# A two-layer adapter and feed-forward kernel: another order of loads, remainders and one fold in its opening

## The reference, cut to what matters

```python
# layer 0, x is 2 x 2048 x 512; domain_id holds one number for each of the 2 batches
hidden = gelu(x @ down_W.T + down_b)                       # 512 -> 128
expert_out = hidden @ expert_W[idx].T + expert_b[idx]      # one expert for each batch
hidden = where(valid, expert_out, hidden) + domain_emb[idx]
x = layernorm(hidden @ up_W.T + up_b + x) * ln_gamma + ln_beta
# layer 1
h = gelu(x @ Wi[e] + bi[e])                                # 512 -> 2048, one expert for each batch
o = h @ Wo[e] + bo[e]                                      # 2048 -> 512
return layernorm(o + x) * gamma[e] + beta[e]
```

## Time and profile before

| what | value |
|---|---|
| median of 3 runs | 768.83 us (768.16 to 769.0) |
| time of the profiled execution | 767.69 us |
| its span (first to last instruction) | 765.9 us |
| PE busy | 755.4 us, 99% of the span |
| DVE busy | 514.1 us, 67% |
| POOL busy | 466.9 us, 61% |
| ACT busy | 348.9 us, 46% |
| share of PE in the chain that ended last | 97% |

### The profile page before, as it was taken

The page is one execution under the profiler, slowest core; times in us unless marked ns, Lnnn a source line. Parts: engine busy times, 40 slices in busy tenths (PEclk is TensorE's granted clock), DMA queues, the critical chain, the costliest instruction groups (busy, mean ns, idle before and its releaser), DMA issues.

```text
span 765.9 us, 9925 instructions
## 1 busy us (share of the span) xinstructions
PE 755.4 (99%) x3388; PEld 626.3 (82%) x3388; DVE 514.1 (67%) x1056; ACT 348.9 (46%) x609; POOL 466.9 (61%) x398
## 2 busy tenths in 40 slices
PE   8999999999999999999999999999999999999996
PEld 6888888888888888888888888888888888888885
DVE  7717855789458883689837888368873789545116
ACT  6554445434544444544454344454354444443440
POOL 5497564775648665395655955558653775646441
PEclk9999999999999999999999999999999999999999
DMA  8940000310012000246211300022000210001001
GB/s 313 393 154 1 1 0 13 112 41 1 1 67 86 14 1 0 69 142 257 88 50 69 97 1 1 1 97 69 1 1 1 68 42 1 0 15 42 0 1 55
DMA packets 17270, 45.36 MB, mean 59 GB/s; under 512 B 2115, under 2 KB 3395, under 8 KB 16324
## 3 DMA queue, kind: packets, MB, share of 16 engines
q1 hardware_dynamic: 16532, 43.94, 16.0%
q10 hardware_dynamic: 688, 0.79, 0.3%
HBM read 36.33 MB, written 8.39 MB: 58 GB/s over the span
## 4 chain that ended last, share of the span: by engine, by line
PE 97%; DVE 1%; POOL 0%; issue 0%; ACT 0%; POOLq 0%; DVEq 0%
PE acc L832 15%; PE acc L830 15%; PE acc L831 15%; PE ps_h L832 15%; PE ps_h L830 15%; PE ps_h L831 15%; PE ps L831 2%; PE ps L830 2%; PE ps L832 2%; PE ps_h L938 1%; DVE rows L753 0%; DVE acc L746 0%; DVE stats L735 0%; PE ps L931 0%; POOL up_b L352 0%
## 5 line engine op out<-in xcount | busy, mean ns | idle before, releaser
L306 POOL TENSOR_TENSOR wi<-w_raw,wi 128x512 fp32r<-128x512 f32 x128 | 168.0, 1313 | 242.9 <-ACT wi L446 242.3
L467 ACT ACTIVATE h<-ps_h,bi_now 128x512 fp32r<-128x512 f32 x110 | 75.9, 690 | 295.0 <-PE ps_h L832 295.0
L657 DVE TENSOR_TENSOR h<-ps_h,h 128x512 fp32r<-128x512 f32 x124 | 85.5, 690 | 167.0 <-ACT ps_h L468 166.0
L830 PE MATMUL acc<-wo,h 128*128 128x512 f32 x504 | 196.1, 389 | 0.0
L831 PE MATMUL acc<-wo,h 128*128 128x512 f32 x504 | 196.1, 389 | 0.0
L832 PE MATMUL acc<-wo,h 128*128 128x512 f32 x504 | 196.1, 389 | 0.0
L830 PE MATMUL ps_h<-x1t,wi 128*128 128x512 f32 (+1 forms) x504 | 195.3, 387 | 0.0
L831 PE MATMUL ps_h<-x1t,wi 128*128 128x512 f32 (+1 forms) x504 | 195.2, 387 | 0.0
L832 PE MATMUL ps_h<-x1t,wi 128*128 128x512 f32 (+1 forms) x504 | 195.2, 387 | 0.0
L312 POOL TENSOR_TENSOR wo<-w_raw,wo 128x512 fp32r<-128x512 f32 x126 | 162.9, 1293 | 0.0
L646 DVE STREAM_TRANSPOSE ps<-rows 32x128 f32<-32x128 f32 x448 | 144.3, 322 | 5.7
(11 more groups left out here) (157 smaller groups left out, 620.3 us busy)
## 6 DMA issues: line engine op xcount, KB each, us to landing
w_raw<-in_w SPq DMA_DIRECT2D x32, 512.0 KB, 9.0
rows<-in_x SPq DMA_DIRECT2D x32, 256.0 KB, 2.8
out<-rows SPq DMA_DIRECT2D x32, 256.0 KB, 2.0
xt_raw<-in_xT SPq DMA_DIRECT2D x7, 1024.0 KB, 4.8
vec<-in_vec SPq DMA_DIRECT2D x2, 768.0 KB, 8.3
xt_raw<-in_xT ACTq DMA_DIRECT2D x2, 256.0 KB, 4.6
xt_raw<-in_xT SPq DMA_DIRECT2D x2, 256.0 KB, 3.6
vec<-in_vec SPq DMA_DIRECT2D x1, 512.0 KB, 6.4
```

The lines of the kernel that those rows point to most:

```text
L306: pool.tensor_tensor(slot[:, 1], w_raw[:, c, 0, :].rearrange("p (k i) -> p k i", k=KD), slot[:, 0].bitcast(F32), ALU.subtract).then_inc(wi ...
L467: act.activation(h_slot(t, c)[:, 0, :], bank, ACT.Gelu, bias=bias)
L657: dve.tensor_tensor(h_slot(t, c)[:, 1, :], hidden_bank(t, c), h_slot(t, c)[:, 0, :].bitcast(F32), ALU.subtract).then_inc(h_split, 1)
L830: pe.matmul(out, left[0], right[0], start=start, stop=False)
```

## The change

The loads of SP are asked for in another order: the up bias ahead of up_W, rows 0 and 1 ahead of parts 2 and 3 of x transposed. Gamma and beta lie in 128 rows of memory, one for each partition, and no longer in one row that is read 128 times. DVE copies the up bias right after the flags, ahead of the remainders; up_W's remainder comes behind that of part 0. The remainder of part 2 goes from DVE to POOL. ACT rounds part 0 before up_W, and parts 2 and 3 after the fold; batch 1's expert bias is put off. The second place of `WARM` goes from 3 to 1. Batch 1's fold is copied once more by ACT (`fold_copy`, in the memory of `up_raw`), and its remainder is taken by POOL in tile 0, behind `up_bias(1)`, instead of by DVE; PE waits for that remainder only at c == 4 of tile 0. POOL takes the second remainder of wi ahead of `add_up_bias(3)`, and the third and fourth ahead of the inverse roots.

```diff
@@ -43,7 +43,7 @@
 WI_RING, WO_RING, H_RING = 4, 4, 4
 
 UP_AT, NORM_AT, TURN_AT, SPLIT_AT = (4, 6, 8, 10), (5, 7, 9, 11), (6, 8, 10, 12), (7, 9, 11, 13)
-WARM = (4, 3, 4)
+WARM = (4, 1, 4)
 EARLY = 4
 LATE = 6
 
@@ -88,6 +88,7 @@
         ones = rows[:, 1, 1, 0:P]
         one_row = rows[:, 1, 2, :]
         up_b_raw = rows[:, 1, 3, :]
+        fold_copy = rows[:, 1, 0, :]
         valid = sb("valid", [P, 3, BATCH])
         ids = sb("ids", [1, 4, BATCH], I32)
         idx = sb("idx", [1, 2, BATCH], I32)
@@ -139,6 +140,7 @@
         flags_ready, flags_spread = sem("flags_ready"), sem("flags_spread")
         down_landed, up_landed, up_b_landed = sem("down_landed"), sem("up_landed"), sem("up_b_landed")
         up_b_spread, up_b_wide, bias_copied = sem("up_b_spread"), sem("up_b_wide"), sem("bias_copied")
+        fold_copied = sem("fold_copied")
         exp_landed = [sem(f"exp_landed{b}") for b in range(BATCH)]
         vec0_landed = sem("vec0_landed")
         bi_landed = [sem(f"bi_landed{b}") for b in range(BATCH)]
@@ -198,9 +200,9 @@
         @block.sync
         def _(sp):
             sp.dma_start(ids[:, 0:2, :], ids_d.rearrange("p (i b) -> p i b", b=BATCH)).then_inc(ids_landed, 16)
+            sp.wait_ge(const_ready, 4)
+            sp.dma_start(one_row[0:1, :], vec0_d[0:1, 0, :]).then_inc(up_b_landed, 16)
             sp.dma_start(up_raw, upW_d).then_inc(up_landed, 16)
-            sp.wait_ge(const_ready, 4)
-            sp.dma_start(one_row[0:1, :], vec0_d[:, 0, :]).then_inc(up_b_landed, 16)
             sp.wait_ge(idx_ready, 1)
 
             def load_exp(b):
@@ -214,12 +216,12 @@
                 sp.dma_start(rows[:, 0, s, :], x_d[0, s, :, :]).then_inc(rows_landed[s], 16)
 
             load_exp(0)
+            first_rows(0)
+            first_rows(1)
             first_xt(2)
-            first_rows(0)
+            first_xt(3)
             load_exp(1)
-            first_xt(3)
-            first_rows(1)
-            sp.dma_start(vec0[:, :, :], vec0_d[:, 1:3, :].to_broadcast([P, 2, D])).then_inc(vec0_landed, 16)
+            sp.dma_start(vec0[:, :, :], vec0_d[:, 1:3, :]).then_inc(vec0_landed, 16)
             first_rows(2)
             first_rows(3)
             sp.wait_ge(idx_ready, 2)
@@ -245,6 +247,7 @@
             sp.wait_ge(valid_ready, 1)
             sp.wait_ge(up_b_wide, 1)
             sp.wait_ge(up_b_ready, 2)
+            sp.wait_ge(fold_split, 2)
             for s in range(SUB):
                 sp.wait_ge(xb_ready, s + 1)
                 sp.dma_start(rows[:, 1, s, :], x_d[1, s, :, :]).then_inc(rows_landed[s], 16)
@@ -354,7 +357,7 @@
             pool.wait_ge(up_b_wide, 1)
             add_raw_bias(0)
             add_raw_bias(1)
-            pool.wait_ge(first_split, 3)
+            first_rest(2)
             first_rest(3)
             inverse_root(0, 0, 0)
             up_bias(0)
@@ -362,12 +365,12 @@
             add_up_bias(0, 0, 2, 0)
             inverse_root(0, 0, 1)
             wi_rest(0, 0)
+            wi_rest(0, 1)
             add_up_bias(0, 0, 3, 0)
-            wi_rest(0, 1)
+            wi_rest(0, 2)
             inverse_root(0, 0, 2)
-            wi_rest(0, 2)
+            wi_rest(0, 3)
             inverse_root(0, 0, 3)
-            wi_rest(0, 3)
             wo_rest(0, 0)
             wo_rest(0, 1)
             pool.wait_ge(ffn_landed[0], 16)
@@ -379,6 +382,9 @@
                         wi_rest(*ahead(t, bt, bu, c + WI_AHEAD)[::2])
                     if c == 1 and isinstance(t, int) and t == 0:
                         up_bias(1)
+                        pool.wait_ge(fold_copied, 1)
+                        pool.tensor_tensor(fold_w[:, 1, 1, :], fold_copy, fold_w[:, 1, 0, :].bitcast(F32),
+                                           ALU.subtract).then_inc(fold_split, 1)
                     if c in (1, 2, 3, 4):
                         if isinstance(t, int) and t == 0:
                             add_out_bias(0, 0, c - 1, 0)
@@ -491,29 +497,31 @@
                 act.wait_ge(bias_done, b + 1)
                 act.activation(up_b[:, b, :], bank, ACT.Copy).then_inc(bias_copied, 1)
 
+            first_round(0)
             act.wait_ge(up_landed, 16)
             act.activation(up_w[:, 0, :], up_raw, ACT.Copy).then_inc(up_w_hi, 1)
-            first_round(0)
             first_round(1)
             expert_round(0)
             expert_bias(0)
-            first_round(2)
             first_hidden(0, half_hi)
             fold_round(0)
             expert_round(1)
+            first_round(2)
             first_round(3)
             copy_bias(0, acc[:, 3, :])
-            expert_bias(1)
             first_hidden(2, hid_hi)
             wi_round(0, 0, 0)
             x1t_round(0, 0, 0)
+            wi_round(0, 0, 1)
             fold_round(1)
-            wi_round(0, 0, 1)
+            act.wait_ge(up_w_ready, 1)
+            act.activation(fold_copy, fold_bank(1), ACT.Copy).then_inc(fold_copied, 1)
             x1t_round(0, 1, 0)
             wi_round(0, 0, 2)
             wi_round(0, 0, 3)
             for c in range(WO_AHEAD):
                 wo_round(0, 0, c)
+            expert_bias(1)
             x1t_round(0, 2, 0)
             x1t_round(0, 3, 0)
             xt_round(1, 0)
@@ -709,18 +717,17 @@
                               ALU.subtract).then_inc(down_w_ready, 1)
             dve.wait_ge(flags_spread, 1)
             dve.tensor_copy(valid[:, 0:2, :], ps0[:, 1, 0:2 * BATCH].rearrange("p (i b) -> p i b", b=BATCH)).then_inc(valid_ready, 1)
+            dve.wait_ge(up_b_spread, 1)
+            dve.tensor_copy(up_b_raw, acc[:, 0, :]).then_inc(up_b_wide, 1)
+            first_rest(0)
             dve.wait_ge(up_w_hi, 1)
             dve.tensor_tensor(up_w[:, 1, :], up_raw, up_w[:, 0, :].bitcast(F32), ALU.subtract).then_inc(up_w_ready, 1)
-            first_rest(0)
             first_rest(1)
             dve.wait_ge(exp_hi, 1)
             dve.wait_ge(valid_ready, 1)
             expert_rest(0)
-            dve.wait_ge(up_b_spread, 1)
-            dve.tensor_copy(up_b_raw, acc[:, 0, :]).then_inc(up_b_wide, 1)
-            first_rest(2)
-            dve.wait_ge(first_split, 3)
-            dve.sem_inc(xt_split, 3)
+            dve.wait_ge(first_split, 2)
+            dve.sem_inc(xt_split, 2)
             first_hid_rest(0, half_hi, half_split)
             fold_rest(0)
             dve.wait_ge(exp_hi, 2)
@@ -766,7 +773,6 @@
             first_hid_rest(2, hid_hi, hid_split)
             first_scale(1)
             x1t_rest(0, 0, 0)
-            fold_rest(1)
             x1t_rest(0, 1, 0)
             adapter_sum(0, 2, 0, acc_part(2))
             first_stats(2)
@@ -871,7 +877,7 @@
                       k == 0, k == KD - 1).then_inc(down_done, 1)
 
             def first_down(j):
-                if j < 3:
+                if j < 2:
                     pe.wait_ge(first_split, j + 1)
                 else:
                     pe.wait_ge(xt_split, j + 1)
@@ -963,15 +969,15 @@
             bias_product(0, acc[:, 3, :]).then_inc(bias_done, 1)
             first_down(2)
             first_down(3)
+            turn(0)
             fold_product(1)
-            turn(0)
             adapter_up(0, 0, 2, acc[:, 2, :])
             turn(1)
             pe.wait_ge(bias_copied, 1)
             adapter_up(0, 0, 3, acc[:, 3, :])
 
             first_early(1)
-            pe.wait_ge(fold_split, 2)
+            pe.wait_ge(fold_copied, 1)
             for c in range(1, EARLY - 1):
                 early_products(c, 1)
             turn(2)
@@ -997,6 +1003,8 @@
                     if more and c in (0, 1):
                         adapter_down(t + 1, 2 * c)
                         adapter_down(t + 1, 2 * c + 1)
+                    if c == 4 and isinstance(t, int) and t == 0:
+                        pe.wait_ge(fold_split, 2)
                     if more and c in UP_AT:
                         s = UP_AT.index(c)
                         if s:
@@ -1042,8 +1050,8 @@
                                np.asarray(L0_cond_expert_b).reshape(E0, A, 1),
                                np.asarray(L0_cond_domain_emb).reshape(E0, A, 1),
                                np.broadcast_to(np.asarray(L0_cond_down_b).reshape(1, A, 1), (E0, A, 1))], axis=2),
-        "vec0": np.stack([np.asarray(L0_cond_up_b), np.asarray(L0_cond_ln_gamma),
-                          np.asarray(L0_cond_ln_beta)]).reshape(1, 3, D),
+        "vec0": np.broadcast_to(np.stack([np.asarray(L0_cond_up_b), np.asarray(L0_cond_ln_gamma),
+                                          np.asarray(L0_cond_ln_beta)]).reshape(1, 3, D), (P, 3, D)),
         "w": np.concatenate([wi, wo], axis=3),
         "bi": np.asarray(L1_cond_bi).reshape(E1, CH, P).transpose(0, 2, 1),
         "vec1": np.stack([np.asarray(L1_cond_bo), np.asarray(L1_cond_gamma),
```

## The result

The changed kernel takes 771.43 us (median of 7 executions, 769.88 to 773.11), the kernel before, run beside it on the same chip, 768.00 us (7 executions, 767.55 to 769.00). The ratio is 1.0045, with a 95% interval of 1.0032 to 1.0058: slower, by 3.4 us. The profiled execution of the changed kernel took 770.88 us, with a span of 769.1 us. Against the profiled execution before that is 3.19 us more, and 3.2 more in the span.

A forecast was written before the change was run, and what follows sets the result against it. PE was taken to bound the kernel, carrying any opening delay to the end. DVE's order (0.7, with 0.1 for a start behind a wait) and POOL's turns (2.2) gave +3.0 on 768.83: 771.8 us, range 769.4 to 773.3.

The forecast's parts named there:

- What bounds the kernel: PE, 99% busy and dense after the opening; any shift in the opening reaches the end one for one.
- PE's part: Two products fewer ahead of the up bias: its spreading starts 0.86 us earlier, of which 0.41 is left.
- DVE's order without POOL: Copy and up_W ahead of part 1's remainder move its end from 7.72 to 9.44 us; +0.8 counts.
- POOL's turns: POOL's two up bias additions alternate with DVE's remainders, moving part 1's end on to 11.63 us: 2.2 us.
- PE's waits: In the opening PE waits 0.6 us for part 0's remainder and 2.6 for part 1's.
- What was costed at nothing: Fold remainder, part 2 on POOL, wi order, transfers and ACT's extra copy: taken as no cost; up to 0.3 us if ACT late.
- One turn only: Rival, chance 0.10: POOL's first addition runs between up_W's and part 1's remainders; +1.9 us, 770.7.
- rows 0 landing ahead of POOL's asking: Transfers in the opening: rows 0 lands near 7.3 us, before POOL asks at 7.85; taken as no cost.
- POOL costs nothing: Rival, chance 0.07: POOL doesn't delay DVE, part 1's remainder ends at 9.44 us; +0.8 us, 769.6.
- faster: Rival, chance 0.08: DVE's list sets the opening's end, so the fold remainder's 0.6 us comes off; 767.4 us.
- no change: Rival, chance 0.08: some of both, with the time within 1.5 us of the kernel before.
- The clock falls: Rival, chance 0.05: PE idle at 9.1 to 11.7 us drops to 1.2 GHz; +2.5 us more, 774.3.

The follow-up runs named there:

- e1: The changed kernel with DVE's copy of the up bias back behind the remainders of part 0, up_W, part 1 and the expert: 767.69 us, ratio 0.9995.
- e5: The kernel before with only the fold part: ACT copies batch 1's fold, POOL instead of DVE takes its remainder: 768.09 us, ratio 0.9996.
- e8: The changed kernel with nine more products keeping PE busy between first_down(0) and first_down(1): 770.48 us, ratio 1.0026.
- e10: The changed kernel unaltered, run once more for one profile: 770.92 us.
- e12: The kernel before with WARM 4, 1, 1, gamma and beta in 128 rows, rows 0 and 1 earlier, parts 2 and 3 later, part 2's remainder on POOL: 767.20 us.
- e3: The kernel before with DVE's copy of the up bias ahead of all remainders, nothing else: 772.25 us, ratio 1.0048.
- e7: From e1: up bias spread behind first_down(1), WARM 4, 3, 0, rounding and remainders in the order part 0, part 1, up_W: 769.03 us, ratio 1.0014.
- e11: The kernel before with WARM 4, 1, 1, five of eleven products that keep PE busy left out: 767.30 us, ratio 0.9992.
- e4: The kernel before with only WARM changed, from 4, 3, 4 to 4, 1, 4: 767.75 us, ratio 0.9995.
- e2: The changed kernel with one more wait: POOL adds the up bias only after part 1's remainder is taken: 768.78 us, ratio 1.0009.
- e6: The kernel before with only gamma and beta in 128 rows of memory: 768.32 us, ratio 0.9999.
- e9: The changed kernel unaltered, run again in five executions: 772.22 us, ratio 1.0051.

## Why the prediction was right

The forecast was 771.8 us, the measurement 771.43; slower had 0.77. Its steps in order, predicted and then measured in the profile of the changed kernel:

- *What bounds the kernel.* "Whatever happens in the opening is carried to the end one for one": fold product +3.24, dense stretch +3.19, profiled time +3.19. Right, in e1 to e5, e8 to e10 and e12 as well (e3 +2.76 and +2.81, e5 +0.98 and +0.95). Not so in e7 and e11, where POOL's additions held DVE behind the fold product: e11's came 1.12 earlier and the profiled time fell by 0.57.
- *PE's part.* L958 at 5.26 (5.27), DVE's copy at 6.95 (7.22). This step was off. It let PE's pace double at 6.54 as before; in this execution both rows of L958 ran slow, and it doubled at about 7.1. Of the 0.41 us to be gained 0.19 came at the product behind L958 (7.16 to 6.97), and 0.12 at the end of the eight rows (8.21 to 8.09). e4 shows that such a gain does come when nothing takes it: 0.25 us at the fold product.
- *DVE's order without POOL.* +0.8 was the term; e2 shows it alone: +0.7 in the medians. In the profiles it is 768.76 - 767.69 = 1.07, with PE at the slow pace until after 8.6 in e2's.
- *POOL's turns,* the largest term: 2.2 predicted, 2.12 measured by e2 against the changed kernel. The step's form is right too. From the start of part 0's remainder to the end of part 1's it had 4.08 us (7.55 to 11.63), and it took 4.03 (7.83 to 11.86); up_W's remainder 1.78 (1.77); POOL's pair 3.23 (3.20). The Trainium skill, SBUF — State Buffer, section Who interferes with whom, is borne out in that the two exclude each other. Its wording that the later one waits for the whole of the first would have given 4.63 us for that stretch; the measured 4.03 keeps the overlap at the edges that the earlier trace rows showed.
- *PE's waits* of 0.6 and 2.6 were 0.56 and 2.31, DVE's of 0.8 ahead of its second `x1t_rest` was 0.78, and PE is dense from 31.57 instead of 31.4.
- *What was costed at nothing.* e5 (fold), e6 (gamma and beta) and e1 (all but the one place in DVE's list) can't be told from the kernel before. Each is within 0.5 us of it. The other order of wi did remove PE's 1.0 us wait for POOL, and PE waited for L760 instead (1.81 us, 0.42 before), as the prediction had it.
- *The rivals.* "One turn only" isn't excluded but happens beside the forecast's case: it came in one of three profiles of the changed kernel, by the mechanism given (rows 0 after 8.1), and cost 0.5 us less, not 1.1, as the expert's remainder took the second turn. The step that had rows 0 landing ahead of POOL's asking was right only in some executions. "POOL costs nothing" falls by e2, "faster" and "no change" by the result. "The clock falls" was given 0.05 and a profiled time of 770.7 + 2.5 = 773.2; three of 13 executions lie at 773.05 to 773.11 with the lowest clocks. By the means of the clock, as worked out under e8 to e10, it was down ahead of the tail in them, and probably for a shorter time in the one at 771.43. So this rival came true in three executions of 13, as far as means can show it, and its chance was too small. The argument against it looked at waits of 0.7 and 1.0 us only; the tail of the kernel before, where the clock leaves 1.00 at 764.2 us, 4.2 us after the last product, was left unread. The Trainium skill, TensorE: Matmul & The Clock Gate, Part 1, has an idle TensorE fall back to 1.2 GHz. The tails agree (0.50). Behind the idle times of 1.14, 2.31 and 2.33 us in the three profiles PE ran at the fast pace, while e3's clock fell 2.0 us after its last product: an idle time of this length has both outcomes.

The median fits the forecast partly by luck, and two shares of it cancel. The forecast laid +3.0 on a median of 768.83, that of three executions. Seven beside the changed kernel gave 768.00, and on it +3.0 makes 771.0; the 1.14 us between the profiled execution and its kernel's median was too large a term (0.1 to 0.9 by the medians of the later runs). And the measured median lies between a lower group whose middle is 770.7 and an upper one at 772.2 to 773.1. The forecast's mechanism alone gives the lower group, which is 2.7 us above the kernel before; the rest of the 3.4 is the slower executions' share.

Open: why the clock falls in some executions and not in others, in which rows the time goes, since no profile caught one, and whether the three at 772.2 to 772.4 are of the same kind.

## What to carry to other kernels

Before an operation is moved ahead in one engine's list, ask whom it releases: here the early copy cost its own engine little and set another engine to take turns with it in the midst of the work for which PE was waiting. An earlier transfer can do the same: in the one profile of the changed kernel in which rows 0 landed later (e9), the execution was 0.5 us faster than in the two others. And an operation that nobody waits for belongs behind those that somebody waits for, even when its input comes first; holding POOL back by one wait (e2) gave back three quarters of the loss, and putting the copy behind the remainders (e1) all of it.

## What was not expected of the hardware

**DVE and POOL alternate instruction by instruction, and DVE pays each time.** Two operations of DVE with two inputs in SBUF took 1.77 and 1.74 us in the changed kernel and 0.69 and 0.68 in e2, with the same starts up to there. A small one suffers nearly as much as a large one: 1.36 us for 0.34 in e9. POOL pays less, 3.20 us for a pair that takes 2.53 alone, and an operation of DVE with an input in PSUM paid nothing (0.70 us beside POOL). That they would alternate was read from the earlier trace rows; that the turn is so exactly repeatable (1.77 and 1.74 in two profiles, 1.76 in a third) was not.

**The clock fell behind an idle time of 2.0 us in one tail and stayed up for 5.3 us in another.** The last product ends at 762.82 us in e3 and the granted clock is at 0.50 from 764.8 on; in e8 it ends at 762.63, and the clock leaves 1.00 at 767.9.

**The moment at which PE's pace doubles isn't fixed.** Eight rows of 128 columns that keep PE busy took 1.05 us before, 1.12 in the changed kernel, 1.78 in e1 and 1.92 in e2 and in e9, although PE's list is the same up to there in the last four. By these rows the pace doubled at about 6.5, 7.1, 8.4, 8.9 and 8.8 us; e9 and the first profile of the changed kernel are the same kernel. The stretch tables show a granted clock of 1.00 throughout, so this start can be read from the rows' durations only. It matters for the time where nothing else holds PE back. e5's lists are the kernel before's up to the fold product. In its profile the pace doubled near 8.5 us, and the fold product came at 10.47 instead of 9.49:

```profile
7.83 1.39 PE L945 MATMUL ps_h<-ident 128*128 128x128 f32 x8
...
10.47 0.40 PE L837 MATMUL ps_h<-up_w,exp_w 128*128 128x512 f32 x1
```

That execution took 768.64 us, 0.95 more than the profiled one before, and its fold product stood 0.98 later. The mean granted clock of an execution doesn't tell this: it was 1.000 here and 0.999 before, and differs by the tail. A forecast from one profile can't be finer than this.
